# Expert blocks of a GNN, attention and MoE layer: products under high weights grouped ahead of those under low weights

## The reference, cut to what matters

```
h = silu(einsum('nd,edf->nef', xf, w1))        # D = F = 1024, E = 8
ye = einsum('nef,efd->ned', h, w2)
routed = einsum('ne,ned->nd', combine, ye)     # combine: the weights of the two chosen experts
```

## Time and profile before

| | |
|---|---|
| time before, median of 3 runs | 1125.26 us (1124.53 to 1127.51) |
| the profiled execution, its device time | 1125.52 us |
| its span, first to last instruction | 1123.5 us |
| TensorE busy | 1104.7 us, 98% of the span |
| VectorE, ScalarE, GpSimd busy | 57%, 43%, 6% |
| granted TensorE clock | 1.000 (2.4 GHz) |
| the stretch of the eight expert blocks, 743.4 to 1092.0 us | 348.6 us |

### The profile page before, as it was taken

The page is one execution under the profiler, slowest core; times in us unless marked ns, Lnnn a source line. Parts: engine busy times, 40 slices in busy tenths (PEclk is TensorE's granted clock), DMA queues, the critical chain, the costliest instruction groups (busy, mean ns, idle before and its releaser), DMA issues.

```text
span 1123.5 us, 16001 instructions
## 1 busy us (share of the span) xinstructions
PE 1104.7 (98%) x6160; PEld 949.7 (85%) x6160; DVE 639.4 (57%) x805; ACT 482.7 (43%) x710; POOL 68.1 (6%) x88
## 2 busy tenths in 40 slices
PE   7999999999999999999999999999999999999998
PEld 5789988777777999878778999888988988888876
DVE  6788836676667664343363632436556555656545
ACT  4323322477788412211223322235646556555550
POOL 3000000000000000000000340200000000000003
PEclk9999999999999999999999999999999999999999
DMA  7222111222322022721004442286576666665647
GB/s 247 75 76 76 40 38 75 75 72 104 105 75 75 2 76 76 259 75 64 12 1 167 132 121 83 81 299 228 211 274 215 239 234 223 242 244 205 237 179 278
DMA packets 76485, 156.97 MB, mean 140 GB/s; under 512 B 7161, under 2 KB 7433, under 8 KB 76433
## 3 DMA queue, kind: packets, MB, share of 16 engines
q1 hardware_dynamic: 64908, 127.30, 32.9%
q10 hardware_dynamic: 7300, 15.41, 3.8%
q0 software_dynamic: 4224, 13.55, 3.8%
HBM read 135.69 MB, written 20.54 MB: 139 GB/s over the span
## 4 chain that ended last, share of the span: by engine, by line
PE 91%; DVE 3%; ACT 2%; DMA 1%; issue 1%; DVEq 0%; POOL 0%; POOLq 0%; SPq 0%; ACTq 0%
PE ps L1627 22%; PE ps L1629 22%; PE ps L1628 21%; PE ps L2031 10%; PE ps L2032 5%; PE ps L1726 2%; PE ps L1666 1%; PE ps L1712 1%; PE ps L1865 1%; PE ps L1866 1%; ACT w_hi L681 1%; PE ps L1934 1%; PE ps L1935 1%; PE ps L1751 1%; DMA y_second<-expert_rows,slots 1%
## 5 line engine op out<-in xcount | busy, mean ns | idle before, releaser
L988 DVE TENSOR_TENSOR w_lo<-w_raw,w_hi 128x2048 fp32r<-128x2048 f32 x108 | 244.9, 2289 | 136.9 <-ACT w_hi L681 132.7
L681 ACT CAST w_hi<-w_raw 128x2048 fp32r<-128x2048 f32 x108 | 203.6, 1911 | 92.7 <-PE ps L1935 36.2
L2031 PE MATMUL ps<-xe,w_hi 128*128 128x448 f32 x512 | 160.9, 375 | 0.0
L2032 PE MATMUL ps<-xe,w_lo 128*128 128x224 f32 x512 | 134.8, 263 | 0.0
L2031 PEld LDWEIGHTS ps<-xe,w_hi 128*128 128x128 f32 x512 | 95.9, 187 | 7.9
L1627 PE MATMUL ps<-w_hi,xt_hi 128*128 128x512 f32 (+1 forms) x240 | 96.8, 403 | 4.7 <-DVE xt_lo L1168 1.4
L1627 PE MATMUL ps<-w_hi,he_hi 128*128 128x512 f32 (+1 forms) x256 | 101.2, 395 | 0.0
L1629 PE MATMUL ps<-w_hi,he_lo 128*128 128x512 f32 (+1 forms) x256 | 100.2, 391 | 0.0
L1628 PE MATMUL ps<-w_lo,he_hi 128*128 128x512 f32 (+1 forms) x256 | 100.0, 390 | 0.0
L2032 PEld LDWEIGHTS ps<-xe,w_lo 128*128 128x128 f32 x512 | 97.5, 190 | 0.4
L1628 PE MATMUL ps<-w_lo,xt_hi 128*128 128x512 f32 (+1 forms) x240 | 94.2, 393 | 0.0
(11 more groups left out here) (326 smaller groups left out, 1994.6 us busy)
## 6 DMA issues: line engine op xcount, KB each, us to landing
w_raw<-in_L_ffn_w SPq DMA_DIRECT2D x64, 1024.0 KB, 5.6
w_raw<-in_L_gnn_W_neigh SPq DMA_DIRECT2D x8, 1024.0 KB, 5.2
w_raw<-in_L_gnn_W_self SPq DMA_DIRECT2D x8, 1024.0 KB, 5.1
w_raw<-in_L_ffn_shared_gate_up SPq DMA_DIRECT2D x8, 1024.0 KB, 7.2
w_raw<-in_L_mix_Wv SPq DMA_DIRECT2D x4, 1024.0 KB, 6.5
w_raw<-in_L_mix_Wk SPq DMA_DIRECT2D x4, 1024.0 KB, 5.2
w_raw<-in_L_mix_Wq SPq DMA_DIRECT2D x4, 1024.0 KB, 5.1
w_raw<-in_L_mix_Wo SPq DMA_DIRECT2D x4, 1024.0 KB, 5.0
```

Source lines behind the costliest of these rows:

```text
L681: copy(w_hi[b][:, s * HK:(s + 1) * HK, :], w_raw[s][:, :, :]).then_inc(hi_done, 1)
L988: V_.tensor_tensor(w_lo[b][:, k, :], w_raw[s][:, :, :], as32(w_hi[b][:, k, :]), ALU.subtract).then_inc(lo_done, 1)
L2031: mat(PS(key)[:, a, 0:2 * B], wh[:, k, w_cols], xe[:, :, k, 0:B], start=k == 0, stop=False)
L2032: last = mat(PS(key)[:, a, 0:B], wl[:, k, w_cols], xe_hi[:, k, 0:B], start=False, stop=k == KF - 1)
```

## The change

Within a unit the products under high weights now come first, and those under low weights after them. For "he" that is sixteen matmuls of 448 columns and then sixteen of 224. For "y" it is sixteen of 512 columns with `w_hi` (`he_hi` and `he_lo` in turn) and then eight with `w_lo`. In the first unit of a job the wait for the whole job is split: ahead of k = 0 and of k = 4 a wait for the high half (`hi_done`), and the wait for the low weights (`lo_done`) between the two groups. The waits for `he` (`lo_out`) stay ahead of k = 4 and k = 6 of ("y", 0, 0). The number of matmuls, their operands and their shapes stay.

```
-                    wh, wl = weights(J_X + h, j)
                     for n in range(h * HK // 2, (h + 1) * HK // 2):
                         ...
                         for a in range(2):
-                            w_cols = ...
                             for k in range(KF):
-                                mat(PS(key)[:, a, 0:2 * B], wh[:, k, w_cols], xe[:, :, k, 0:B], start=k == 0, stop=False)
-                                last = mat(PS(key)[:, a, 0:B], wl[:, k, w_cols], xe_hi[:, k, 0:B], start=False, stop=k == KF - 1)
+                                wh = high_weights(J_X + h, k) if first and a == 0 else w_hi[(J_X + h) % 2]
+                                mat(PS(key)[:, a, 0:2 * B], wh[:, k, cols_of[a]], xe[:, :, k, 0:B], start=k == 0, stop=False)
+                        if first:
+                            weights(J_X + h, j)
+                        for a in range(2):
+                            for k in range(KF):
+                                last = mat(PS(key)[:, a, 0:B], w_lo[(J_X + h) % 2][:, k, cols_of[a]], xe_hi[:, k, 0:B],
+                                           start=False, stop=k == KF - 1)
...
-                    weights(J_X + 2 + h, j)
                     for s in range(BC):
                         ...
-                        by_tokens(key, PS(key)[0:BROWS[s], 0, :], HE, J_X + h, slice(s * 128, s * 128 + BROWS[s]),
-                                  arrives=(lambda k: j * BR + nth[("he", k // 2)] if k % 2 == 0 and k >= KF // 2 else None)
-                                  if h == s == 0 else None).then_inc(ready[slot(key)], 1)
+                        for k in range(KF):
+                            wh = high_weights(job, k) if s == 0 else w_hi[job % 2]
+                            if h == s == 0 and k % 2 == 0 and k >= KF // 2:
+                                pe.wait_ge(lo_out, j * BR + nth[("he", k // 2)])
+                            mat(out_ap, he_hi[:, k, of_rows], wh[:, k, :], start=k == 0, stop=False)
+                            mat(out_ap, he_lo[:, k, of_rows], wh[:, k, :], start=False, stop=False)
+                        if s == 0:
+                            weights(job, j)
+                        for k in range(KF):
+                            last = mat(out_ap, he_hi[:, k, of_rows], w_lo[job % 2][:, k, :], start=False, stop=k == KF - 1)
+                        last.then_inc(ready[slot(key)], 1)
```

More of the change, by code:

```diff
@@ L2022, in _, with high_weights @@
                 pe.wait_ge(lo_out, j * BR + R0)
+                def high_weights(job, k):
+                    if k % HK == 0:
+                        pe.wait_ge(hi_done, j * 8 + (2 * job + k // HK + 1))
+                    return w_hi[job % 2]
                 for h in range(2):
-                    wh, wl = weights(J_X + h, j)
                     for n in range(h * HK // 2, (h + 1) * HK // 2):
-                        key = ("he", n)
+                        key, first = ("he", n), n == h * HK // 2
                         claim(key, j)
+                        cols_of = [slice((2 * n + a) % HK * 128, ((2 * n + a) % HK + 1) * 128) for a in range(2)]
                         for a in range(2):
-                            w_cols = slice((2 * n + a) % HK * 128, ((2 * n + a) % HK + 1) * 128)
                             for k in range(KF):
-                                mat(PS(key)[:, a, 0:2 * B], wh[:, k, w_cols], xe[:, :, k, 0:B], start=k == 0, stop=False)
-                                last = mat(PS(key)[:, a, 0:B], wl[:, k, w_cols], xe_hi[:, k, 0:B], start=False, stop=k == KF - 1)
+                                wh = high_weights(J_X + h, k) if first and a == 0 else w_hi[(J_X + h) % 2]
[6 more added lines that the diff above has]
+                                           start=False, stop=k == KF - 1)
                         last.then_inc(ready[slot(key)], 1)
@@ L2043, in _ @@
                 for h in range(2):
-                    weights(J_X + 2 + h, j)
+                    job = J_X + 2 + h
                     for s in range(BC):
@@ L2047, in _ @@
                         claim(key, j)
-                        by_tokens(key, PS(key)[0:BROWS[s], 0, :], HE, J_X + h, slice(s * 128, s * 128 + BROWS[s]),
-                                  arrives=(lambda k: j * BR + nth[("he", k // 2)] if k % 2 == 0 and k >= KF // 2 else None)
-                                  if h == s == 0 else None).then_inc(ready[slot(key)], 1)
+                        of_rows, out_ap = slice(s * 128, s * 128 + BROWS[s]), PS(key)[0:BROWS[s], 0, :]
+                        for k in range(KF):
[9 more added lines that the diff above has]
+                        last.then_inc(ready[slot(key)], 1)
                         if h == s == 0:
```

## The result

The changed kernel took 1128.53 us in the median of 7 runs (1126.67 to 1130.17), the kernel before 1124.54 us on the same chip. The ratio on record is 1.0025, 95% interval 1.0013 to 1.0037: 2.8 us slower, of an expected 2.5. (The two medians lie 4.0 us apart, still inside that interval, which reaches from 1.5 to 4.2 us.) The result lies 0.7 us above the forecast of 1127.8 us and inside the range of 1125 to 1131. The two terms behind that number do not hold, though. Each was off by 2 us, in opposite directions.

The account below looks back on a forecast made before the run. TensorE, never idle in the eight expert blocks, bounds the kernel. An earlier wait for unit 3 (+3.6 us) and grouped "he" pairs (-1.1) sum to +2.5, so 1127.8 us, 0.2% slower, range 1125.0 to 1131.0.

Parts of the forecast that it names:

- The term that decided, the wait at k = 6: In ("y", 0, 0), the wait for unit 3's he_lo comes six matmuls sooner and stalls every block: +3.6 us.
- The chain of unit 3 starts from the end of 'he' on TensorE.: Where he_lo's timing starts; claimed it moves along with TensorE, so the lateness doesn't grow from block to block.
- The lateness as read: he_lo of unit 3 against the new due time of k = 6: 0.08 to 0.54 us late, 1.93 together.
- The latency: From the end of VectorE's releasing instruction to the start of TensorE's matmul: 0.10 us taken per block.
- the restart: Slower pace of some ten matmuls on TensorE after a wait: 0.11 us more per block.
- The pairs: 512 pairs of 448 and 224 columns in units "he": grouping gives 0 to -2.3 us, taken as -1.1.
- a short one 0.109 again, a long one 0.200 to 0.205: Start-to-start us of grouped 224- and 448-column matmuls in "he", the short one set by its successor's load.
- The outer upper bound: Pairs in "he" at 0.109 + 0.212 us: 0.0073 more a pair, +3.7 us.
- the choice of one load ahead: TensorE's weight loads go no further ahead than one matmul, against the skill's reorder window of 64; gives -1.1 us.
- Costly grouping: Rival: runs of sixteen short matmuls in "he" expose their loads, pairs +3.7 us, 1132.6 us in all; chance 0.13.
- The hidden wait: Rival: the wait for unit 3 in ("y", 0, 0) stays free, leaving -1.1 us, about 1124.2; chance 0.12.
- The gain from dropping the alternation: Rival: alternation in "he" itself costs time and grouping frees it, -7 us, 1121.9 us in all; chance 0.05.

Follow-up runs that it names:

- e3: Whole change, but four low products (k = 0 to 3) of ("y", 0, 0) moved ahead of the wait at k = 6; blocks' stretch 349.53 us, ratio 1.0026.
- e4: Whole change, but ("y", 0, 0) waits for unit 3 of "he" already at k = 4; blocks' stretch 359.9 us, ratio 1.010.
- e10: Whole change, with two more matmuls of 448 columns at the start of unit 3 of "he" in each block; blocks' stretch 352.79 us.
- e11: The kernel before itself, unchanged, under another name; blocks' stretch 348.58 us, ratio 1.0006.
- e2: Kernel before with only the units "y" grouped, "he" still alternating; blocks' stretch 351.01 us, ratio 1.0018.
- e9: Whole change, but "he" goes two high, two low products in turn; units "he" 5.04 to 5.06 us each.

## Why the prediction was right, and where it was not

**The bound, and what the change could free: right.** Before, TensorE had no idle time in the blocks, and after, no wait for `w_hi` or `w_lo` appears there. The wait that moved was over in either place.

**The term that decided, the wait at k = 6: right in place and kind, twice the size.** It stalls in all eight blocks, at the matmul named, and e3 and e4 tie it to the number of matmuls ahead. The sum said 3.6 us; it measured 1.76. Two steps failed.
- *"The chain of unit 3 starts from the end of 'he' on TensorE."* It starts at the end of unit 1 (13.74 to 13.75 us from there to `he_lo`, in e10 too). The two units in between take 0.064 us longer when grouped, and TensorE reaches ("y", 0, 0) later by that, while the data does not. So the floor fell from 2.93 to 2.86 us, 0.5 us in eight blocks, a part of the other term given back here.
- *The lateness as read.* The 1.93 us of the earlier trace rows held four blocks in which the data came later than the floor by 0.13 to 0.45 us; the same kernel had none in e11, so I call it chance in the loads. The longest differences, 0.54 and 0.43, came from there. At the floor of e11 the eight differences sum to 8 x 0.09 = 0.7 us. In the profiled execution after no block was late. It was right that such lateness costs where it comes: the late blocks of e2 and e4 show it at full price.
- The latency was 0.055 us and not the 0.10 of the earlier trace rows, the restart 0.14 and not the 0.11 of the earlier trace rows. Together they are close to the 0.21 that was used. With the floor, 8 x (2.86 + 0.055 - 2.84 + 0.14) = 1.7 us, against the 1.76 measured.

The forecast that the stall would be longest in the fourth and fifth block was wrong for the same reason: it was a property of one execution.

**The pairs: wrong sign.** Forecast -1.1 us between 0 and -2.3, measured +0.95. The failed step is "a short one 0.109 again, a long one 0.200 to 0.205". The long one was 0.204, inside; the short one behind a short one was 0.111 to 0.112, more than the pace of bare loads, which I had taken as the value. That the split of a pair into 0.109 and 0.205 was wrong could be seen before the change: by the starts of the earlier trace rows a short matmul costs 0.10 and a long one 0.21, and the trace has 0.100 and 0.213 in the mean. The 0.109 of a load is no lower bound for a short matmul where the two alternate, and the prediction had used it as one against the 0.10. The outer upper bound, 0.0073 more for a pair, covered the result; 0.0019 came on average. The row behind the choice of one load ahead holds after the change too: in the grouped streams each load starts 2 to 10 ns behind the start of the matmul ahead of its own, and never before it. So the sign was missed with that reading right.

**Rivals.** Costly grouping had the right sign and a quarter of its price (0.95 us for 3.7). Its stated cause, loads exposed in a run of sixteen, is not shown: runs of two cost as much (e9). The hidden wait did not happen. The gain from dropping the alternation had the parts half right, since the long matmul fell from 0.213 to 0.204, but the short one rose by more: alternating is the cheaper order.

**The total.** +3.6 - 1.1 = +2.5 stands against +1.76 + 0.95 = +2.7. The errors of -1.8 and +2.05 cancelled. The number was right by luck, its parts were not.

No version has a shorter stretch than the kernel before. e3 removes the stall and keeps the dearer pairs; undoing these as well leaves the order of before.

## What to carry to other kernels

A wait is worth moving only if TensorE arrives at it early; where the profile shows no idle time, look at what a new order does to the waits that are free today, and count the matmuls that stood ahead of each. Before pricing such a wait, follow the data back to what its chain really starts from, on every engine in order, and read its margin from more than one execution: the floor is the steady price, and what lies above it changes from execution to execution. A stall shorter than the overlap of two matmuls is in no list of waits; compare starts. Before whole runs are compared for a difference of 1 us, sort them by their mean granted clock, and read a mean clock of a stretch together with the starts in it.

## What the runs showed of the hardware that I had not expected

- Matmuls of 448 and 224 columns, each with a load of its own, take 0.3133 us a pair in strict alternation and 0.3154 in runs of sixteen, as in runs of two. A short one takes 0.100 to the next start in the alternation and 0.111 in runs of sixteen.
- A stall of 0.08 us costs 0.22: the first start after it comes 0.34 us later and not 0.23, and the next ones at up to 0.24. The Trainium skill, "TensorE: Matmul & The Clock Gate" (Back-to-back issue gap), gives N/2.4 + 2.5 ns as the isolated gap, some 216 ns for 512 columns, and 131 ns as what a stream of loads and matmuls sustains there. Here such a stream, with a load for each, ran at 227 in the median, above both, and the measurement decides.
- The same instructions ahead of the experts took 742.2 to 745.5 us from one execution to the next. In the three with 745.35 or more (after, e2, e3) the granted clock was at half once more around 227 to 231 us, where it cost the kernel after 1.7 us; in the other ten that was not so. The mean clock of the first 45 us does not order them: the six at 0.96 began at 742.2 to 742.5 and the four at 1.00 at 743.05 to 743.43, because the 1.00 leaves out a start that has no clock on record.
